# A private 4 KB tile for the rounding step: narrower pieces, moved staging buffers and two waits less in an eight-core transformer layer

## What is computed

```python
def _weight_quant(w):
    scale = 1.0 / jnp.clip(jnp.mean(jnp.abs(w)), 1e-05)
    return jnp.clip(jnp.round(w * scale), -1.0, 1.0) / scale
def _act_quant(x):
    scale = 127.0 / jnp.clip(jnp.max(jnp.abs(x), axis=-1, keepdims=True), 1e-05)
    return jnp.clip(jnp.round(x * scale), -128.0, 127.0) / scale
def _bitlinear(x, w):
    return jnp.einsum('bsi,oi->bso', _act_quant(x), _weight_quant(w))
def ffn(x):
    return _bitlinear(_silu(_bitlinear(x, w_gate)) * _bitlinear(x, w_up), w_down)
x = x + 0.5 * ffn(_layernorm(x))
x = x + attn(_layernorm(x))     # K, Q, K2 projections, three cumsums over the tokens, a projection
x = x + 0.5 * ffn(_layernorm(x))
```

## Time and profile before

| | us |
|---|---|
| timed runs, median of two | 6713.02 (6707.91 to 6718.13) |
| the profiled execution, device time | 6673.8 |
| its span on core 1, first to last instruction | 6672.8 |
| spans of the eight cores | 6592.8 to 6672.8 |
| mean granted TensorE clock of core 1, share of full speed | 0.798 |
| TensorE busy | 4002.2 (60%) |
| VectorE busy | 2470.9 (37%) |
| ScalarE busy | 1490.7 (22%) |
| GpSimd busy | 488.7 (7%) |

### The profile page before, as it was taken

The page is one execution under the profiler, slowest core; times in us unless marked ns, Lnnn a source line. Parts: engine busy times, 40 slices in busy tenths (PEclk is TensorE's granted clock), DMA queues, the critical chain, the costliest instruction groups (busy, mean ns, idle before and its releaser), DMA issues.

```text
span 6672.8 us, 54064 instructions; the slowest of 8 cores (6592.8 to 6672.8 us)
## 1 busy us (share of the span) xinstructions
PE 4002.2 (60%) x19026; PEld 2110.9 (32%) x19026; DVE 2470.9 (37%) x3687; ACT 1490.7 (22%) x1760; POOL 488.7 (7%) x505
## 2 busy tenths in 40 slices
PE   0007637875568647576367755686475763777467
PEld 0004413333233323334133332333233341333323
DVE  4653164123532244231641235322442315422452
ACT  2113113122131221231131221312212311312212
POOL 0100120001100020001200011000200002000200
PEclk6559868787789868788688877898687986899688
DMA  7993622325224343235224253253432352232532
GB/s 228 293 272 95 116 48 82 133 85 92 76 66 155 72 73 107 80 104 119 51 77 135 86 89 77 62 158 73 73 108 76 107 112 53 82 126 89 89 88 89
DMA packets 229207, 699.80 MB, mean 105 GB/s; under 512 B 22096, under 2 KB 22096, under 8 KB 224848
## 3 DMA queue, kind: packets, MB, share of 16 engines
q10 hardware_dynamic: 110592, 402.70, 19.2%
q0 software_dynamic: 76576, 159.41, 13.3%
q1 hardware_dynamic: 41776, 134.24, 6.4%
HBM read 788.55 MB, written 41.94 MB: 124 GB/s over the span
## 4 chain that ended last, share of the span: by engine, by line
PE 42%; DVE 23%; DMA 14%; ACT 13%; issue 7%; POOL 1%; DVEq 1%; ACTq 0%; SPq 0%; POOLq 0%
PE PB L601 11%; PE PB L606 11%; PE PB L683 9%; DMA sarena<-sc_d 8%; PE PB L753 5%; PE PB L403 5%; DVE pool L571 3%; ACT pool L434 2%; DMA sarena<-sc_u 2%; ACT poolb L438 2%; ACT pool L642 2%; ACT pool L769 1%; DVE smal L577 1%; ACT pool L568 1%; ACT pool L515 1%
## 5 line engine op out<-in xcount | busy, mean ns | idle before, releaser
L601 PE MATMUL PB<-sarena,poolb 128*128 128x512 bf16 x4096 | 1593.6, 389 | 338.1 <-DMA sarena<-sc_u 236.4
L606 PE MATMUL PB<-sarena,poolb 128*128 128x512 bf16 x4096 | 1591.8, 389 | 0.0
L683 PE MATMUL PB<-sarena,poolb 128*128 128x512 bf16 x4096 | 959.9, 393 | 212.2 <-DMA sarena<-sc_d 211.7
L403 PE MATMUL PB<-ident,pool 128*128 128x128 f32 x2464 | 476.5, 357 | 959.8 <-ACT pool L515 365.9
L571 DVE SCALAR_TENSOR_TENSOR pool<-PB,smal,pool 128x512 f32<-128x512 f32 x512 | 382.0, 746 | 1345.1 <-ACT pool L568 1345.1
L403 PEld LDWEIGHTS PB<-ident,pool 128*128 128x128 f32 x2464 | 416.0, 192 | 988.1 <-issue 988.1
L601 PEld LDWEIGHTS PB<-sarena,poolb 128*128 128x128 bf16 x4096 | 408.0, 100 | 912.1 <-issue 493.0
L568 ACT ACTIVATE pool<-PB,smal 128x512 f32<-128x512 f32 x512 | 326.3, 684 | 1437.6 <-PE PB L606 1408.0
L683 PEld LDWEIGHTS PB<-sarena,poolb 128*128 128x128 bf16 x4096 | 399.6, 100 | 768.4 <-issue 370.9
L606 PEld LDWEIGHTS PB<-sarena,poolb 128*128 128x128 bf16 x4096 | 407.8, 100 | 481.1 <-issue 60.4
L753 PE MATMUL PB<-poolb 128*128 128x256 bf16 x3072 | 413.7, 303 | 169.1 <-ACT pool L769 125.2
(11 more groups left out here) (139 smaller groups left out, 2961.0 us busy)
## 6 DMA issues: line engine op xcount, KB each, us to landing
sarena<-sc_g ACTq DMA_DIRECT2D x256, 512.0 KB, 4.3
sarena<-sc_u ACTq DMA_DIRECT2D x256, 512.0 KB, 5.5
sarena<-sc_d ACTq DMA_DIRECT2D x256, 512.0 KB, 3.9
pool<-wgt SPq DMA_DIRECT2D x32, 1024.0 KB, 10.0
pool<-wut SPq DMA_DIRECT2D x32, 1024.0 KB, 9.3
pool<-wdt SPq DMA_DIRECT2D x32, 1024.0 KB, 10.3
poolb<-wk1t POOLq DMA_DIRECT2D x64, 512.0 KB, 8.1
poolb<-wq1t POOLq DMA_DIRECT2D x64, 512.0 KB, 7.9
```

The lines of the kernel that those rows point to most:

```text
L403: TE.transpose(out=PB[:, b * 1024 + j * 128: b * 1024 + (j + 1) * 128], in_=s_, identity=ident[:, :])
L601: TE.matmul(out=pb[ttg * 4 + (tt % 2)][:, :], lhsT=aq[:, tt, ic, :], rhs=gsl[:, bsel * 2048 + ic4 * 512: bsel * 2048 + (ic4 + 1) * 512], s ...
L606: tl_ = TE.matmul(out=pb[ttg * 4 + 2 + (tt % 2)][:, :], lhsT=aq[:, tt, ic, :], rhs=usl[:, bsel * 2048 + ic4 * 512: bsel * 2048 + (ic4 + 1) ...
L683: tl_ = TE.matmul(out=pb[tt * 2 + obk][:, :], lhsT=hq[:, tt, ic, :], rhs=dsl[:, bsel * 2048 + ic2 * 1024 + obk * 512: bsel * 2048 + ic2 * ...
```

## The change

The int32 tile gets its own memory: `qi32`, 128x1024, half for VectorE, half for ScalarE. Four things follow from its size and place.
- Groups of the rounding transposes shrink from eight blocks to four, in `emit_ffn_pre` (four groups become eight) and in the hidden-tile calls (four groups become eight per token tile). Plain copies keep eight.
- `tern_piece` rounds a 128x2048 piece in four strips of 512 columns, each with both instructions; a staging buffer is free after the last of the eight instructions instead of after L299.
- Staging buffers 2 and 3 move to `pool` columns 16392 to 20488.
- Two waits go: ScalarE's wait for VectorE's opening-stage work ahead of the first `gu_load`, and VectorE's wait for ScalarE ahead of the three small copies (L790 to L792) in `emit_half_mms`.

```diff
-    qi32 = pool.bitcast(I32)
-    qiV = qi32[:, 16392:17416]
-    qiS = qi32[:, 17416:18440]
-    qiT = qi32[:, 18440:20488]
+    qi32 = E(nc.sbuf_tensor("qi32", [128, 1024], I32))
+    qiV = qi32[:, 0:512]
+    qiS = qi32[:, 512:1024]
...
-           pool[:, 4096:6144], pool[:, 6144:8192]]
+           pool[:, 16392:18440], pool[:, 18440:20488]]
...
-        cV.wait(V)
-        ti = qiT[:, 0:pf]
-        cV.inc(V.tensor_scalar(out=ti, in0=buf, scalar1=dcol, scalar2=None,
-                               op0=ALU.add))
-        tw_state["slotV"][bsel] = (cV, cV.n)
-        cV.wait(V)
         prev = tw_state["stgV"][bsel]
         if prev is not None:
             prev[0].wait(V, prev[1])
-        cV.inc(V.tensor_scalar(out=sbf, in0=ti, scalar1=nm128_ap, scalar2=None,
-                               op0=ALU.add))
+        for j0 in range(0, pf, 512):
+            cV.wait(V)
+            cV.inc(V.tensor_scalar(out=qiV[:, 0:512], in0=buf[:, j0:j0 + 512],
+                                   scalar1=dcol, scalar2=None, op0=ALU.add))
+            cV.wait(V)
+            cV.inc(V.tensor_scalar(out=sbf[:, j0:j0 + 512], in0=qiV[:, 0:512],
+                                   scalar1=nm128_ap, scalar2=None,
+                                   op0=ALU.add))
+        tw_state["slotV"][bsel] = (cV, cV.n)
...
-               for ic in range(DC)],
-              aq[:, tt, :, :]) for tt in range(TT)], evac="submagic")
+               for ic in range(q4 * 4, q4 * 4 + 4)],
+              aq[:, tt, q4 * 4:q4 * 4 + 4, :])
+             for tt in range(TT) for q4 in range(2)], evac="submagic")
...
-            for s_, n_ in tern_done["v"]:
-                s_.wait(S, n_)
...
-                   for ic in range(q * 8, q * 8 + 8)],
-                  hq[:, tt, q * 8:q * 8 + 8, :]) for q in range(4)],
+                   for ic in range(q * 4, q * 4 + 4)],
+                  hq[:, tt, q * 4:q * 4 + 4, :]) for q in range(8)],
...
-                cS.wait(V)
                 cV.wait(V)
                 V.tensor_copy(out=xn2T[:, :, 0], in_=xnc)
```

More of the change, by code:

```diff
@@ L183, in build_nc @@
     cV.wait(V)
-    cV.inc(V.tensor_copy(out=qi32[:, 16392:16393], in_=dcol))
+    cV.inc(V.tensor_copy(out=qi32[:, 0:1], in_=dcol))
     cV.wait(V)
-    cV.inc(V.tensor_scalar(out=t1[:, 0:1], in0=qi32[:, 16392:16393],
+    cV.inc(V.tensor_scalar(out=t1[:, 0:1], in0=qi32[:, 0:1],
                            scalar1=-2.0, scalar2=-1.0,
@@ L418, in transpose_quads @@
                     cV.wait(V)
+                    assert w_ <= 512
                     cV.inc(V.tensor_scalar(out=qiV[:, 0:w_], in0=pt,
@@ L1111, in build_nc @@
     tern_done["gu"] = [(x, x.n) for x in dTG + dTU]
-    tern_done["v"] = [(cV, cV.n)]
     tern_done["d"] = [(x, x.n) for x in dTD]
```

## The result

| | before | after |
|---|---|---|
| median of the timed runs, us | 6685.4 (10 runs) | 6798.9 (11 runs) |
| ratio, 95% interval | | 1.0135 [1.0098, 1.0172] |
| slowest core's span in the profile, us | 6672.8 | 6766.1 |
| mean span of the eight cores, us | 6628.2 | 6731.3 |
| mean start of the first gate matmul, eight cores, us | 488.0 | 569.9 |

What follows compares the result with a forecast made beforehand. No engine was taken to bound the whole (TensorE 42% of the chain), so each edit was priced in its stage. 94 + 3 - 10 + 30 - 4 = +113 on 6713.0 gave 6826 us; own range 6790 to 6860, overall 6775 to 6882.

Steps and rivals of the forecast that it cites:

- strips: Opening stage: 512-column VectorE instructions of 486 ns plus 0.106 us gap add 1.95 us to each of 48 pieces, +94.
- later release: Opening stage: staging buffers come free 1.4 us later, which may show at two changes to the next weight's mean, +3.
- first gate load: End of opening stage: loads move ahead into the last ternary pass, first gate matmul waits only for VectorE, -10.
- groups: Rounding transposes: half-width ScalarE pairs cost +1.6 us per FFN and +0.3 per input-path call, 16 of each, +30.
- small copies: Before TensorE's projection matmuls: copies run beside ScalarE's copy, TensorE starts 0.5 us earlier in eight chunks, -4.
- rival 2: Transpose calls: half-wide groups halve the end drain, waits of 5.33 us fall to 2.7, -128, 6668 us; chance 0.05.
- Rival 1: Opening stage: 512-column VectorE strips cost 692 ns like other such rows, +173 instead of +94, 6905 us; chance 0.08.
- rival 3: Transpose groups: a 0.37 us handoff stall appears in half of the new pairs, +89, 6885 us; chance 0.15.
- rival 4: Opening stage: a strip's fixed part is the one-column row's 154 ns, +68 instead of +94, 6800 us; chance 0.06.

Runs made afterwards that it cites:

- the run without the first wait: Kernel before without ScalarE's wait for VectorE's opening-stage work ahead of the first gate load; ratio 0.9979 [0.9949, 1.0009].
- the run without waits: Kernel before at full width, int32 values in idle memory, both waits of the change gone; ratio 0.9972 [0.9938, 1.0006], -19 us.
- full-width pieces: Changed kernel with weight pieces rounded at full width, int32 values written over the staging buffer; ratio 1.0009 [0.9973, 1.0044], +6 us.
- the run with that call wide: Kernel before with four-block groups everywhere except the first hidden-tile call of each FFN; ratio 1.0010 [0.9973, 1.0046].
- the groups alone: Kernel before with groups of four blocks instead of eight in the rounding transposes, nothing else; ratio 1.0033 [1.0001, 1.0064], +22 us.

## Why the prediction was right, point by point

The forecast of +113 us (ratio 1.0168) lies in the measured interval, 1.0098 to 1.0172, near its upper end. By its terms, measured in the mean of the cores:

| step | predicted | measured |
|---|---|---|
| strips | +94 | +90.2 (three passes, 359.0 against 268.9) |
| later release | +3 | +0.7 (two stretches between passes, 106.1 against 105.4) |
| first gate load | -10 | -8.0 (1.0 us behind VectorE instead of 9.0) |
| groups | +30 | +28 (16 x (1.45 + 0.30), cores 1, 3 and 6; +30 over all eight) |
| small copies | -4 | -5 |
| sum | +113 | +106 |

The spans give +103.1 in the mean; a first pass that happens to start 1.0 us earlier is in it. The timed runs give +90 (66 to 115). Every term is in the right place, all but the release (lost in the spread of the cores) show with the right sign, and no large errors cancel. The terms behind the first gate matmul rest on the timelines: the span from there to the end moves by some 10 us between executions of the same code (6140.2 before, 6126.5 in the run without the first wait).

- The strips: duration and gap as predicted (486 ns, 0.108 us). The term is 4 us too large because a wait went that I had not priced. Before, L306 had a gap of 0.18 us in the earlier trace rows, 8.6 us over 48 pieces in its group, against 0.11 for its neighbours. It waits for VectorE and then for an old store. The first four pieces have no old store to wait for, and there the gap before L306 is 0.11. The loop puts the store's wait ahead of the first strip instruction, where it passes while L294 still runs, and the gap of 0.18 is gone. Theory and rows agree: 0.07 x 44 pieces with an old store = 3 us.
- The release: this term was mis-sized. At full width the price may be there (1.3 and 1.7 us in the run without waits, 0.6 and 1.0 with full-width pieces); with strips it is +0.7 in all, which can't be told from nothing, since the same stretch varies between 51.4 and 54.9 us over the cores of the kernel before. That the slower pieces leave the loads more room (DMA share 0.77 for 0.93) is the likely reason. My 1.4 was the size for the wrong kernel.
- The first gate load: right in the place and in what is late next. The 10.7 us from VectorE's last small instruction to the matmul were those of the slowest core; the mean was 8.5, or 9.0 from the end of the last piece.
- The groups: the first call of an FFN pays, as said, and the run with that call wide shows it. The sizes were close (688 and 722 ns on 690 and 720), the +1.5 of the first call came out exactly, and the later calls shrink as said, by 0.25 instead of 0.1 to 0.2; the end of the stretch grew by 0.6 instead of 0.3. Two readings were wrong. I expected TensorE's waits for the evacuation to stay near 5 us each; they fell to 3, rival 2's own mark, without its gain. And TensorE stops after five of eight groups, not after half.
- Rival 1 falls with 486 ns, rival 2 with the groups alone, rival 3 with the same run (+28 to +30 in the traces, not +89), rival 4 with the line through four widths. The trace of before could have excluded rival 3 already: I took the stall of 0.37 us from two pairs, but of all 1280 pairs of its eight cores 16 have one. In the changed kernel it is 16 of 2560.
- The page "VectorE: DVE Perf Modes" of the Trainium skill, in its section on the perf-mode tier table, gives fp32 `tensor_scalar` on SBUF the doubled rate, in a row for 2048 elements with 1227 ns. The trace agrees: L294 takes 1227 ns, and the rate of the strips' form holds at smaller widths too, 0.52 ns a column down to 256.
- The Trainium skill's "Perfetto Trace Analysis", section "Optimizing Scalar/DVE Operations", gives about 60 ns of engine-busy overhead per VectorE instruction on SBUF and about twice that in profiled latency. By these an estimate for the 288 instructions more is 17 or 35 us; measured are 90. In this chain of dependent instructions each one more costs 0.22 + 0.11 us.

## What to carry to other kernels

Price a split by the fixed part and the gap of one dependent instruction (here 0.33 us on VectorE), times its count, and ask first whether the engine is the bound of that stage; memory for an intermediate may be had in a buffer that is idle just then, here the input that it replaces, which brought 85 us back. A wait that shrinks in the list of waits is no gain until the stretch around it is shorter: measure from one fixed event to the next. Where one engine holds all of a pre-step ahead of a pipeline, try moving or interleaving the pre-step before tuning the pipeline's width.

## What the runs showed that I had not expected

- The order of two waits ahead of one instruction matters: with the wait that is long satisfied put second, the instruction starts 0.18 us after its predecessor (44 of 48 pieces); without that wait, or with it put first, ahead of the first strip instruction, 0.11.
- At full width the ternary passes have little room for other loads (DMA share 0.93): with the first gate and up loads moved to its start, the last pass is 2 to 4 us longer, and with a buffer released 1.4 us later the stretch behind a pass is 0.6 to 1.7 us longer. With pieces of 7.5 us neither shows beyond 1 us.
